# A Macaron block with routed experts on one core: shared expert moved into routing, expert rows scattered by token

## The chip, the cores and the metric

The kernel runs on one NeuronCore of one Trainium2 chip. The metric is the device time of one execution in microseconds (us). PE is TensorE, PEld its weight loads, DVE VectorE, ACT ScalarE, POOL GpSimd, SP the sync engine, which here only issues DMAs. An L with a number is a line of the kernel before.

## What is computed

4096 tokens (4 x 1024) of 256 float32 features pass a mixture-of-experts feed-forward, causal attention with 16 heads, and the same feed-forward again. The change touches the feed-forward alone:

```python
x = x + 0.5 * ffn(layernorm(x)); x = x + attention(layernorm(x)); x = x + 0.5 * ffn(layernorm(x))
# ffn(xf), T tokens, D = 256, 8 experts, TOP_K = 2, MOE_FF = 176, SHARED_FF = 352
scores = sigmoid(xf @ gate_w.T)
topk_w, topk_idx = top_k(scores, 2); topk_w = 2.5 * topk_w / topk_w.sum(-1)
shared_out = silu(xf @ shared_wg.T) * (xf @ shared_wu.T) @ shared_wd.T
h = silu(einsum('td,efd->etf', xf, exp_wg)) * einsum('td,efd->etf', xf, exp_wu)
all_out = einsum('etf,edf->etd', h, exp_wd)
routed_out = (topk_w[..., None] * all_out[topk_idx, arange(T)[:, None]]).sum(1)
return shared_out + routed_out
```

## The kernel before, in words

Tokens lie in 32 tiles of 128 partitions; X stays in SBUF through the whole kernel. Nearly float32 accuracy on TensorE comes from splitting each operand in a rounded high part (float32r, written by ACT) and the rest, the low part (DVE or POOL): every product is made in three passes, high x high, high x low, low x high (`split_passes`, L557). So each operand costs one pass of ACT and one of another engine.

A feed-forward (L92) has three stages with a barrier of all engines between them.

**Routing** (L120 to L550). Eight windows of four tiles: DVE normalises (L387), ACT stores the normalised rows to DRAM (L328), PE transposes them (L505), ACT and DVE split (L306, L392), PE makes the logits (L515, L522). Meanwhile ten weight units (two shared, eight experts) are loaded by SP through two raw buffers (L245, L249), rounded by ACT (L313, L322) and subtracted by POOL (L275, L283); all stay in SBUF. Then comes a chain on DVE, each link waiting for the one before (L417 to L477): the two best experts of each token, the counts (with two products, L540), and a slot for each token and choice in a list of 72 tiles of 128 rows sorted by expert. Eight rounds of one-hot matrices (DVE L485 and L489, ACT L353, POOL L293, PE L547) turn this into the token number of each slot.

**Expert stage** (L562). For each of the 72 tiles POOL gathers 128 rows of the normalised tokens by an indirect DMA (L604, four buffers, each waiting for the transposes of the tile four before), PE transposes (L701), six passes of 352 columns go up (L711), silu and product (L644, L672), two transposes of 88 columns (L720), six passes of 256 columns go down (L731), ACT copies (L623), and SP stores the tile at its slots (L613). The expert's weights are picked by a number loaded into a register.

**Shared stage** (L758). For each of the 32 token tiles: normalise and transpose again (L858, L938), twelve passes of 352 columns (L948), three transposes of h (L957), nine passes of 256 columns (L968). POOL gathers the two expert rows of each token from DRAM (L811, four tiles deep, waiting for the sum of the tile four before), DVE adds them with their weights (L879) and then the shared result (L886); the first feed-forward also takes the statistics for the next layer norm (L892), the second stores the result (SP, L821).

The order of the work on each engine is the order of the calls in its block; nothing is reordered.

Of the kernel before, what the change touches and what calls it, by code (L numbers as in the profile page):

```python
# [73 lines left out]
class Shapes:  # L74
    def __init__(self, x, w_up, w_down, gate):
# [9 lines left out]
        self.FH = self.FF // 2  # L85
# [3 lines left out]
        assert self.NS == 2 and self.NC == 2 and 2 * self.FH == self.FF and P // 2 < self.FH <= P and self.NT % 4 == 0 and self.NJ % 4 == 0  # L89


def feed_forward(nc, tag, S, X, ST, MV, ident, w_up, w_down, w_shared, gate, xn_dram, y_dram, out_dram):  # L92
# [4 lines left out]
    D, NT, NU, NS, FF, E, NJ, FH = S.D, S.NT, S.NU, S.NS, S.FF, S.E, S.NJ, S.FH  # L97
    NG = NT * TOP_K
    with ExitStack() as ctx:
# [3 lines left out]
        WUh = sb("WUh", [P, 2, NU * 2 * FF], F32R)  # L103
        WUl = sb("WUl", [P, 2, NU * 2 * FF], F32R)
        WDh = [sb(f"WDh{c}", [FH, E * D], F32R) for c in range(2)]
        WDl = [sb(f"WDl{c}", [FH, E * D], F32R) for c in range(2)]
        WSh = sb("WSh", [P, 3, D], F32R)
        WSl = sb("WSl", [P, 3, D], F32R)
        RSTD = sb("RSTD", [P, NT])
        W12 = sb("W12", [P, TOP_K, NT])  # L110
        slots_u = sb("slots_u", [P, TOP_K, NT], U32)
        tok_u = sb("tok_u", [P, NJ], U32)
        unit_i = sb("unit_i", [P, NJ], I32)
        X2 = X[:, :, :].rearrange("p t d -> p (t d)")
        MV2 = MV[:, :, :].rearrange("p t s -> p (t s)")
        NW = NT // 4
        assert NW <= NU <= NW + 2


        with ExitStack() as c1:  # L120
            sem = semaphores(nc, c1, f"{tag}1")

            def sb1(name, shape, dt=F32):
                return c1.enter_context(nc.sbuf_tensor(f"{tag}1_{name}", shape, dt))

            def ps1(name, shape):
                return c1.enter_context(nc.psum_tensor(f"{tag}1_{name}", shape, F32))

            XN = sb1("XN", [P, 2, 4, D])
            xh = sb1("xh", [P, 2, 2, 4 * P], F32R)  # L130
            xl = sb1("xl", [P, 2, 2, 4 * P], F32R)
            GW = sb1("GW", [P, 2, E])
            GWhl = sb1("GWhl", [P, 2, 2 * E], F32R)
            GWh0 = sb1("GWh0", [P, 2, 2 * E], F32R)
            LT = sb1("LT", [2 * E, 2, 4 * P])
            ADD = sb1("ADD", [2 * E, E])
            stage = sb1("stage", [P, 2, 4 * FF])
            stageD = sb1("stageD", [P, 2, 2, D])
            ps_x = [ps1(f"ps_x{i}", [P, 512]) for i in range(4)]
            ps_gate = ps1("ps_gate", [P, NT * E])  # L140
            ps_lt = [ps1(f"ps_lt{i}", [2 * E, 512]) for i in range(2)]
            ps_count = ps1("ps_count", [P, 2, E * NT])
            ps_tok = ps_x[0][:, 0:2 * NJ]
            SC = sb1("SC", [P, NT, E])
            SC2 = sb1("SC2", [P, NT, E])
            EQ = sb1("EQ", [P, NT, E])
            PR = sb1("PR", [P, NT, E])
            OH = sb1("OH", [P, TOP_K, NT, E])
            SEL = sb1("SEL", [P, E, NT], BF16)
            M12 = sb1("M12", [P, TOP_K, NT])  # L150
            PMAX = sb1("PMAX", [P, NT])
            DEN = sb1("DEN", [P, NT])
            prio_i = sb1("prio_i", [P, E], I32)
            prio = sb1("prio", [P, E])
            lower_t = sb1("lower_t", [P, P], BF16)
            ones_b = sb1("ones_b", [P, P], BF16)
            ones_f = sb1("ones_f", [P, E * NT])
            CUM = sb1("CUM", [P, E, NT])
            EXC = sb1("EXC", [P, E, NT])
            SLOT = sb1("SLOT", [P, E, NT])  # L160
            CNT = sb1("CNT", [P, E])
            CNTi = sb1("CNTi", [P, E], I32)
            NTI = sb1("NTI", [P, E])
            CT = sb1("CT", [P, E])
            BASE = sb1("BASE", [P, E])
            SL = sb1("SL", [P, TOP_K, NT])
            SLi = sb1("SLi", [P, TOP_K, NT], I32)
            Ri = sb1("Ri", [P, NG], I32)
            Ti = sb1("Ti", [P, NG], I32)
            RF = sb1("RF", [P, NG])  # L170
            TF = sb1("TF", [P, NG])
            row_i = sb1("row_i", [P, P], I32)
            row_f = sb1("row_f", [P, P])
            row_b = sb1("row_b", [P, P], BF16)
            par_i = sb1("par_i", [P, 1], I32)
            par_f = sb1("par_f", [P, 1])
            GE = sb1("GE", [P, NJ, E])
            UF = sb1("UF", [P, NJ])
            tile_of = sb1("tile_of", [P, NG])

            CH = NG // 8
            RSEL = sb1("RSEL", [P, 2, CH, P], BF16)
            EQT = sb1("EQT", [P, 2, CH, NJ], BF16)
            TSEL = sb1("TSEL", [P, 2, CH, 2, NJ], BF16)
            tokf = sb1("tokf", [P, 2 * NJ])

            raw_in = [sem("raw_in0"), sem("raw_in1")]
            gate_in = sem("gate_in")
            consts = sem("consts")
            chain = sem("chain")  # L190
            weights_hi = sem("weights_hi")
            split_w = sem("split_w")
            rstd_in = sem("rstd_in")
            rstd_out = sem("rstd_out")
            stats_done = sem("stats_done")
# [1665 lines left out]
```

## Time and profile before

| | us |
|---|---|
| median of 3 runs | 1437.1 (1436.49 to 1438.13) |
| the profiled execution | 1431.21 |
| its span, first to last instruction | 1429.5 |
| PE busy / DVE busy / ACT busy / POOL busy in it | 1219.7 / 1019.7 / 770.1 / 547.7 |
| mean granted clock of TensorE | 0.903 |

The profile comes from one execution. The granted clock is in parts of 2.4 GHz; 0.50 is 1.2 GHz. Busy time of POOL's indirect DMAs is the time in which it writes their descriptors, not that of the transfer. The span holds three parts that follow on each other: first feed-forward, attention, second feed-forward.

### The profile page before, as it was taken

The page shows a single profiled execution, that of the slowest core. Times are in us where ns is not written, and L with a number is a line of the kernel's source. Part 1 is how long each engine was busy: PE and PEld are TensorE (multiplying, and loading weights), DVE is VectorE, ACT ScalarE, POOL GpSimd, SP SyncE. Part 2 cuts the span into 40 slices and gives each one's busy share as a digit, 9 for nine tenths or more (in the row PEclk, how much of TensorE's full clock was granted, in tenths as well). Part 3 has the DMA queues.
Part 4 walks back from the last instruction along what each step waited for, and adds up shares of the span by engine and source line. Part 5 has one row for each costly group of instructions (what it writes and reads, how often), then busy time and mean ns, then how long its engine had stood idle before and what let it go on. Part 6 is the DMA issues. An engine that isn't in the chain of part 4 may idle for free. (4 is left out here: it accounts for less than half of the span.)

```text
span 1429.5 us, 42640 instructions
## 1 busy us (share of the span) xinstructions
PE 1219.7 (85%) x14356; PEld 938.2 (66%) x14357; DVE 1019.7 (71%) x2317; ACT 770.1 (54%) x1965; POOL 547.7 (38%) x745
## 2 busy tenths in 40 slices
PE   2817999899969849999998999997865299998998
PEld 1516999899958714555554555553743199998998
DVE  6594555479979688898886888981766845554887
ACT  2524556433336504887775777877544156564333
POOL 1555444245524401332332223222535554442554
PEclk9557999999979958999998999999975599998999
DMA  5602433322254492221221222101244034442333
GB/s 184 189 16 76 125 123 122 94 67 73 74 169 166 177 114 52 67 63 59 60 63 49 59 59 64 45 4 35 95 135 135 1 119 124 123 120 76 108 111 106
DMA packets 94745, 132.12 MB, mean 92 GB/s; under 512 B 15040, under 2 KB 79488, under 8 KB 94592
## 3 DMA queue, kind: packets, MB, share of 16 engines
q1 hardware_dynamic: 73088, 85.97, 21.0%
q0 software_dynamic: 13056, 35.67, 9.0%
q10 hardware_dynamic: 8448, 8.39, 1.7%
q8 instruction: 103, 1.69, 0.5%
q14 instruction: 50, 0.41, 0.1%
HBM read 81.35 MB, written 48.23 MB: 91 GB/s over the span
## 5 line engine op out<-in xcount | busy, mean ns | idle before, releaser
L1467 ACT ACTIVATE s_PR<-s_ps_b 128x512 f32<-128x512 f32 (+3 forms) x768 | 331.2, 496 | 144.8 <-PE s_ps_b L1583 139.9
L1489 DVE TENSOR_REDUCE s_MX<-s_ps_a 128x1 f32<-128x512 f32 (+3 forms) x608 | 358.3, 655 | 54.7 <-PE s_ps_a L1558 51.7
L1583 PE MATMUL s_ps_b<-s_QO,s_KO 99*32 99x512 bf16 (+3 forms) x3072 | 220.0, 329 | 9.2 <-issue 4.4
L1443 POOL TENSOR_SCALAR_AFFINE_SELECT s_PR<-s_PR 128x256 f32<-128x256 f32 x256 | 103.0, 405 | 311.6 <-ACT s_PR L1467 305.6
L1558 PE MATMUL s_ps_a<-s_KO,s_QO 96*32 96x512 bf16 (+3 forms) x3072 | 216.4, 339 | 2.7 <-issue 1.7
L604 POOL DMA_INDIRECT f_XG<-xn_scratch,f_tok_u x144 | 136.4, 947 | 165.5 <-PE f_ps_x L701 155.6
L811 POOL DMA_INDIRECT f_YG<-y_scratch,f_slots_u x128 | 121.0, 945 | 143.5 <-DVE X L886 87.9
L1600 PE MATMUL s_ps_o<-s_PR,s_VG 128*17 128x512 f32 (+3 forms) x1536 | 161.1, 488 | 1.0 <-POOL s_PR L1443 0.6
L1583 PEld LDWEIGHTS s_ps_b<-s_QO,s_KO 99*32 99x32 bf16 x3072 | 82.9, 96 | 91.0 <-ACT s_PR L1467 44.7
L657 DVE TENSOR_TENSOR f_xl<-f_ps_x,f_xh 128x256 fp32r<-128x256 f32 x144 | 61.1, 425 | 97.9 <-ACT f_xh L629 97.9
L1558 PEld LDWEIGHTS s_ps_a<-s_KO,s_QO 96*32 96x32 bf16 x3072 | 84.4, 99 | 69.6 <-DVE s_MX L1489 22.7
L844 ACT ACTIVATE f_SG<-f_ps_u 128x176 f32<-128x176 f32 x128 | 40.6, 317 | 142.3 <-PE f_ps_u L948 142.3
L1553 PE MATMUL s_ps_a<-s_neg,s_identb 128*32 128x128 bf16 (+2 forms) x1408 | 95.4, 253 | 25.1 <-DMA s_KO<-qk_scratch 22.1
L711 PE MATMUL f_ps_u<-f_WUh,f_xh 128*128 x288 | 106.4, 369 | 1.3 <-issue 1.0
L711 PE MATMUL f_ps_u<-f_WUl,f_xh 128*128 x288 | 94.1, 327 | 0.0
L711 PE MATMUL f_ps_u<-f_WUh,f_xl 128*128 x288 | 93.9, 326 | 0.0
L672 DVE TENSOR_TENSOR f_H<-f_SG,f_ps_u 128x176 f32<-128x176 f32 x144 | 48.7, 338 | 62.4 <-ACT f_SG L644 62.4
L948 PE MATMUL f_ps_u<-f_WUh,f_xh 128*128 128x352 f32 x256 | 91.2, 356 | 2.0 <-DVE f_xl L863 2.0
L731 PE MATMUL f_ps_y<-f_WDh,f_hh 88*128 x288 | 92.6, 321 | 0.1
L948 PE MATMUL f_ps_u<-f_WUh,f_xl 128*128 128x352 f32 x256 | 85.3, 333 | 0.0
L948 PE MATMUL f_ps_u<-f_WUl,f_xh 128*128 128x352 f32 x256 | 84.9, 332 | 0.0
L623 ACT ACTIVATE f_YS<-f_ps_y 128x256 f32<-128x256 f32 x144 | 55.3, 384 | 53.8 <-PE f_ps_y L731 53.8
(206 smaller groups left out, 3048.9 us busy)
## 6 DMA issues: line engine op xcount, KB each, us to landing
y_scratch<-f_YS SPq DMA_DIRECT2D x144, 128.0 KB, 1.7
qk_scratch<-p_QK SPq DMA_DIRECT2D x32, 384.0 KB, 2.6
s_QO<-qk_scratch SPq DMA_DIRECT2D x96, 128.0 KB, 2.8
s_KO<-qk_scratch SPq DMA_DIRECT2D x96, 128.0 KB, 2.8
xn_scratch<-f_XN ACTq DMA_DIRECT2D x16, 512.0 KB, 3.3
f_stage<-in_w_up SPq DMA_DIRECT2D x20, 352.0 KB
X<-in_x SPq DMA_DIRECT2D x4, 1024.0 KB, 9.4
x_scratch<-X SPq DMA_DIRECT2D x1, 4096.0 KB, 14.8
```

The source lines that it names most:

```text
L604: nc.gpsimd.indirect_dma_start(out=XG[:, j % 4, :], out_offset=None, in_=xn_dram[:, :], in_offset=bass.IndirectOffsetOnAxis(ap=tok_u[:, j: ...
L711: last = nc.tensor.matmul(ps_u[k % 2][:, 0:2 * FF], xs[a][:, k % 2, c * P:(c + 1) * P], W_up[b][:, c, ds(unit * (2 * FF), 2 * FF)], start= ...
L731: last = nc.tensor.matmul(ps_y[k % 2][:, 0:D], hs[a][:, k % 2, c * P:(c + 1) * P], W_down[b][c][:, ds((unit - NS) * D, D)], start=i == 0, ...
L811: nc.gpsimd.indirect_dma_start(out=YG[:, t % 4, c, :], out_offset=None, in_=y_dram[:, :], in_offset=bass.IndirectOffsetOnAxis(ap=slots_u[: ...
L948: last = nc.tensor.matmul(ps_u[s][:, 0:2 * FF], xs[a][:, k % 2, c * P:(c + 1) * P], W_up[b][:, c, s * 2 * FF:(s + 1) * 2 * FF], start=i == ...
L1443: nc.gpsimd.affine_select(out=tile, in_=tile, compare_op=ALU.is_ge, fill=0.0, base=0, pattern=[[0, 2], [1, P]], channel_multiplier=-1)\
L1467: nc.scalar.activation(PR[:, u // 2 % SLOTS, u % 2, 0:W - lo], ps_b[u % RING][:, lo:W], ACT.Exp, scale=SCALE).then_inc(exp_done, 1)
L1489: nc.vector.tensor_reduce(MX[:, h:h + heads, i, s], ps_a[slot][:, 0:heads * keys].rearrange("p (h n) -> p h n", h=heads), AX.X, ALU.max).t ...
L1553: nc.tensor.matmul(scores[strip, :, keys - P:keys], identb[:, strip], neg[:, 0:heads, :], start=True, stop=False, skip_group_check=True)
L1558: last = nc.tensor.matmul(ps_a[slot][strip, at:at + keys], QO[k][0:R, h, i * P + strip.start:i * P + strip.stop], KO[k][0:R, h, s * W:s * ...
L1583: last = nc.tensor.matmul(ps_b[u % RING][strip, lo:W], KO[k][0:RM, h, i * P + strip.start:i * P + strip.stop], QO[k][0:RM, h, hf * W + lo: ...
L1600: last = nc.tensor.matmul(ps_o[32 * h:32 * h + V1, lo:W], VG[k][:, i, h * V1:(h + 1) * V1], PR[:, (2 * n + h // 2) % SLOTS, h % 2, 0:W - l ...
```

## The change

**Expert tiles are scattered.** The token list now carries, for each slot, the token plus 4096 times the choice (a third column in the one-hot product marks used slots; unused ones get a spare row behind). POOL writes each finished expert tile by an indirect DMA to that row of a DRAM table. SP has nothing to do in the expert stage.

**The shared expert moves into the routing stage**, now `front_stage`. Its products are turned round: the weights are the stationary operand and 512 tokens move, so h comes out transposed and needs no transposes. The normalised x is transposed once, into the room where the expert weights will lie: window w occupies the place of expert w, whose weights are loaded through one raw buffer, and rounded and split, after window w is done. The gate work of all eight windows is ahead of or inside windows 0 and 1; the DVE chain lies in windows 2 and 3, the eight rounds of one-hot work in windows 4 to 7. ACT makes the ids of a round in nine operations; POOL makes none, but two of three low halves of h. SP stores the normalised rows.

**Five passes down.** h of an expert tile is cut 112 + 64 in place of 88 + 88. The low half of the 64 rows lies in partitions 64 to 127 under the high half, and the high weights stand twice, so one pass makes two products.

**The combine stage** has no products: SP loads windows of 512 tokens of both choices (RING = 4), DVE adds.

```diff
@@ expert stage, GpSimd
+            def scatter(j):
+                pool.wait_ge(y_copied, j + 1)
+                nc.gpsimd.indirect_dma_start(
+                    out=pairs_dram[:, :], out_offset=bass.IndirectOffsetOnAxis(ap=dst_u[:, j:j + 1], axis=0),
+                    in_=YS[:, j % 4, :], in_offset=None).then_inc(y_out[j % 4], 16)
+            for j in range(4):
+                gather(j)
+            for j in range(NJ + 3):
+                if j + 4 < NJ:
+                    gather(j + 4)
+                if j >= 3:
+                    scatter(j - 3)
             for k in range(4):
-                sp.wait_ge(y_out[k], 16 * (NJ // 4))
+                pool.wait_ge(y_out[k], 16 * (NJ // 4))
-            for j, k in steps(sp, NJ, 4):
-                sp.wait_ge(y_copied, j + 1)
-                sp.dma_start(y_dram[ds(j * P, P), :], YS[:, k, :]).then_inc(y_out[k], 16)
@@ expert stage, VectorE (h_low) and TensorE (down)
+                nc.vector.tensor_tensor(hl[:, k % 2, :], ps_h[k % 2][0:FA, 0:P],
+                                        hh[0:FA, k % 2, 0:P].bitcast(F32), ALU.subtract).then_inc(hl_done, 1)
+                nc.vector.tensor_tensor(hh[FB:2 * FB, k % 2, P:2 * P], ps_h[k % 2][0:FB, P:2 * P],
+                                        hh[0:FB, k % 2, P:2 * P].bitcast(F32), ALU.subtract).then_inc(hl_done, 1)
+                plan = ((hh[0:FA, b, 0:P], S.AH), (hh[0:FA, b, 0:P], S.AL), (hl[:, b, :], S.AH),
+                        (hh[:, b, P:2 * P], S.BH), (hh[0:FB, b, P:2 * P], S.BL))
@@ front stage
+    GATED = {-1: (0, 1), 0: (2, 3, 4), 1: (5, 6, 7)}
+    LAST_GATED = max(GATED)
+    COUNT_AT = LAST_GATED + 2
+    ROWS_AT = {4: (0, 1), 5: (2, 3), 6: (4, 5), 7: (6, 7)}
+    RING = 3
+            def up(w, m):
+                n = HC * w + m
+                at, used = CHUNKS[m]
+                for a in range(2):
+                    place = take("up" if a else "gate", n)
+                    for i, (c, x, b) in enumerate(split_passes(2)):
+                        last = nc.tensor.matmul(place[0:used, :], WU[b][:, c, a, at:at + used],
+                                                x_part(x, w)[:, c, :], start=i == 0, stop=i == 5)
+                    last.then_inc(up_done, 1)
@@ front stage, TensorE's order in window w
...
+                up(w, 0)
...
+                for n in ROWS_AT.get(w - 1, ())[1:2]:
+                    tokens(n)
+                if w == COUNT_AT:
+                    counts()
+                if w >= 1:
+                    for i in range(4):
+                        down(w - 1, i)
...
+                up(w, 1)
...
+                up(w, 2)
...
+                for n in ROWS_AT.get(w, ())[0:1]:
+                    tokens(n)
@@ front stage, SP: one raw buffer
+            def load_expert(e):
+                if e == 0:
+                    sp.wait_ge(shared_lo, 2 + HC)
+                else:
+                    sp.wait_ge(expert_lo, 3 * e)
@@ front stage, ScalarE
+            def token_ids(n):
+                act.wait_ge(onehot, n + 1)
+                if n >= 2:
+                    act.wait_ge(tok_done, n - 1)
+                nc.scalar.activation(TSEL[:, n % 2, :, 0, :], TSEL[:, n % 2, :, 2, :], ACT.Copy, scale=par_f[:, :])
+                for g in range(CH):
+                    last = nc.scalar.activation(TSEL[:, n % 2, g, 1, :], TSEL[:, n % 2, g, 2, :], ACT.Copy,
+                                                scale=float(n * CH + g))
+                last.then_inc(ids, 1)
@@ front stage, VectorE's order in window w
...
+                gated_h(w, 0)
...
+                if w >= 1:
+                    add_shared(w - 1)
+                if w == LAST_GATED + 1:
+                    choose(0)
+                if w == COUNT_AT:
+                    place()
+                for n in ROWS_AT.get(w, ())[0:1]:
+                    one_hot(n)
...
+                gated_h(w, 1)
...
+                if w == COUNT_AT:
+                    slots(0)
+                gated_h(w, 2)
...
+                h_low_2(w)
+                if w == LAST_GATED + 1:
+                    choose(1)
+                    weigh()
+                if w == COUNT_AT:
+                    slots(1)
+                    divide()
+                    units()
+                for n in ROWS_AT.get(w, ())[1:2]:
+                    one_hot(n)
@@ combine stage, SP and VectorE
+                    sp.dma_start(YG[:, w % RING, c, :, :],
+                                 pairs_dram[at:at + 4 * P, :].rearrange("(i p) d -> p i d", p=P)
+                                 ).then_inc(loaded[w % RING], 16)
+                nc.vector.scalar_tensor_tensor(X[:, t, :], YG[:, t // 4 % RING, c, t % 4, :], W12[:, c, t:t + 1], X[:, t, :],
+                                               ALU.mult, ALU.add).then_inc(x_done if c else mixed, 1)
```

## Rows read from the trace of the kernel before

**Rows 1.** Busy time by stretch: routing, expert, shared stage, second feed-forward.
```profile
core 0: us, PE busy (x) PEld busy (x) DVE busy (x) ACT busy (x) POOL busy (x), PEclk, DMA share, GB/s
18.70:117.07 98.37, 50.36 (x226) 33.47 (x226) 69.82 (x168) 38.93 (x83) 48.08 (x44) 0.61 0.33 98
117.07:281.20 164.13, 156.49 (x1152) 151.30 (x1152) 80.56 (x216) 93.73 (x289) 68.24 (x72) 0.97 0.38 116
281.20:404.82 123.62, 117.40 (x832) 115.38 (x832) 103.89 (x289) 43.12 (x128) 60.50 (x64) 0.97 0.24 68
1042.70:1429.50 386.80, 322.27 (x2210) 299.30 (x2210) 248.38 (x641) 175.92 (x500) 176.50 (x179) 0.87 0.35 107
```

**Rows 2.** Groups of lines, expert stage: busy, mean ns, idle before and its releasers.
```profile
L604 POOL DMA_INDIRECT f_XG<-xn_scratch,f_tok_u x68 | 64.3, 945 | 78.4 <-PE f_ps_x L701 78.1 <-issue 0.3
```

**Rows 3.** Timeline at the expert stage's start: start, us, engine, operation, idle before.
```profile
117.07 1.15 POOL L604 DMA_INDIRECT f_XG<-xn_scratch,f_tok_u  x1 [3.79 <-POOLq L64]
118.52 0.94 POOL L604 DMA_INDIRECT f_XG<-xn_scratch,f_tok_u  x1 [0.30 <-issue]
...
120.00 0.69 PE L701 MATMUL f_ps_x<-ident,f_XG 128*128 128x128 f32 x2 [5.46 <-DMA f_XG<-xn_scratch,f_tok_u]
...
126.86 0.94 POOL L604 DMA_INDIRECT f_XG<-xn_scratch,f_tok_u  x1 [0.81 <-PE f_ps_x L701]
```

**Rows 4.** Timeline: successive TensorE products with 512 and with 256 columns.
```profile
441.72 0.40 PE L1213 MATMUL p_ps_qk<-p_xh,p_Wh 128*128 128x512 f32 x1
...
441.95 0.40 PE L1213 MATMUL p_ps_qk<-p_xl,p_Wh 128*128 128x512 f32 x1
...
357.40 0.28 PE L968 MATMUL f_ps_y<-f_WSh,f_hl 128*128 128x256 f32 x1
...
357.51 0.28 PE L968 MATMUL f_ps_y<-f_WSh,f_hh 128*128 128x256 f32 x1
```

**Rows 5.** Groups of lines, first routing stage (0 to 117 us).
```profile
L275 POOL TENSOR_TENSOR f_WUl<-f_stage,f_WUh 128x704 fp32r<-128x704 f32 x10 | 17.0, 1697 | 33.6 <-ACT f_WDh L322 21.2 <-ACT f_WSh L322 12.4
...
L485 DVE TENSOR_TENSOR f_EQT<-f_row_f,f_TF 128x576 bf16<-128x576 f32 x8 | 12.7, 1582 | 0.0
...
L489 DVE TENSOR_TENSOR f_RSEL<-f_row_f,f_RF 128x1024 bf16<-128x1024 f32 x8 | 9.7, 1212 | 0.0
...
L353 ACT ACTIVATE f_TSEL<-f_EQT,f_par_f 128x576 bf16<-128x576 bf16 x8 | 6.2, 775 | 24.8 <-DVE f_EQT L485 24.8
L336 ACT ACTIVATE f_LT<-f_ps_lt 16x512 f32<-16x512 f32 x8 | 4.7, 586 | 9.9 <-PE f_ps_lt L515 9.9
```

**Rows 6.** Timeline of the first routing stage, rows picked over its second half.
```profile
67.81 0.39 SPq L245 DMA_DIRECT2D f_stage<-in_w_up  x1
...
71.66 0.79 ACT L313 ACTIVATE f_WUh<-f_stage 128x704 fp32r<-128x704 f32 x1 [1.48 <-DMA f_stageD<-in_w_down]
...
77.06 1.27 DVE L430 TENSOR_TENSOR f_SEL<-f_OH 128x256 bf16<-128x256 f32 x1
...
91.08 0.76 DVE L485 TENSOR_TENSOR f_EQT<-f_row_f,f_TF 128x576 bf16<-128x576 f32 x1
...
114.92 0.23 DVE L495 SCALAR_TENSOR_TENSOR f_tok_u<-f_tokf 128x72 uint32<-128x72 f32 x1
```

**Rows 7.** Groups of lines, first shared stage (281 to 405 us).
```profile
L879 DVE SCALAR_TENSOR_TENSOR X<-f_YG,f_W,X 128x256 f32 x48 | 22.9, 478 | 0.0
```

**Rows 8.** Timeline: VectorE's statistics back to back, and its first normalisations.
```profile
6.59 2.71 DVE L1808 BATCH_NORM_STATS2 ST<-X 128x6 f32<-128x256 f32 x8 [6.59 <-DMA X<-in_x]
...
23.93 1.71 DVE L387 TENSOR_SCALAR f_XN<-X,MV,f_RSTD 128x256 f32<-128x256 f32 x5
```

**Rows 9.** Busy time by stretch: cold expert start; output stage (two).
```profile
122.00:126.00 4.00, 3.72 (x16) 3.62 (x16) 1.19 (x3) 2.37 (x4) 2.78 (x3) 0.57 0.34 101
1028.00:1032.00 4.00, 3.39 (x26) 2.93 (x26) 3.45 (x11) 2.46 (x7) 0.00 (x0) 1.00 0.00 0
1000.00:1004.00 4.00, 3.47 (x18) 3.18 (x18) 0.51 (x2) 1.87 (x6) 2.26 (x1) 0.66 1.08 365
```

More of the change, by code:

```diff
@@ L84, in __init__ @@
         self.NJ = self.T * TOP_K // P + self.E
-        self.FH = self.FF // 2
+        self.FB = P // 2
+        self.FA = self.FF - self.FB
+        self.UH, self.UL = 0, 4 * self.FF
+        self.AH, self.AL, self.BH, self.BL = [8 * self.FF + n * self.D for n in range(4)]
+        self.BLOCK = 8 * self.FF + 4 * self.D
         self.HD = 16
@@ L101, in sb @@
             return ctx.enter_context(nc.sbuf_tensor(f"{tag}_{name}", shape, dt))
[L103 to L108, printed above, removed]
+        W = sb("W", [P, E, S.BLOCK], F32R)
         RSTD = sb("RSTD", [P, NT])
         W12 = sb("W12", [P, TOP_K, NT])
-        slots_u = sb("slots_u", [P, TOP_K, NT], U32)
+        dst_u = sb("dst_u", [P, NJ], U32)
@@ L437, in _, with place @@
                                                         ALU.mult, ALU.mult))
+            def place():
                 dve.wait_ge(pre_copied, 2)
@@ L541, in _ @@
                 nc.tensor.matmul(ps_count[:, 1, :], ones_b[:, :], sel, start=True, stop=True).then_inc(pre_done, 1)
-                for n in range(8):
-                    pe.wait_ge(rows, n + 1)
-                    pe.wait_ge(par_ids, n + 1)
-                    pe.wait_ge(tile_ids, n + 1)
-                    for g in range(CH):
-                        last = nc.tensor.matmul(ps_tok, RSEL[:, n % 2, g, :],
-                                                TSEL[:, n % 2, g, :, :].rearrange("p a j -> p (a j)"),
-                                                start=n == 0 and g == 0, stop=n == 7 and g == CH - 1)
-                    last.then_inc(tok_done, 1)
@@ L553, in feed_forward, with tokens @@
-        expert_stage(nc, tag, S, ident, WUh, WUl, WDh, WDl, tok_u, unit_i, xn_dram, y_dram)
-        shared_stage(nc, tag, S, X, ST, MV, RSTD, W12, slots_u, ident, WUh, WUl, WSh, WSl, y_dram, out_dram)
+            def tokens(n):
+                pe.wait_ge(rows, n + 1)
+                pe.wait_ge(ids, n + 1)
+                for g in range(CH):
+                    last = nc.tensor.matmul(ps_tok, RSEL[:, n % 2, g, :],
+                                            TSEL[:, n % 2, g, :, :].rearrange("p a j -> p (a j)"),
+                                            start=n == 0 and g == 0, stop=n == 7 and g == CH - 1)
+                last.then_inc(tok_done, 1)
@@ L557, in split_passes, with expert_stage @@
+            for i in range(4):
+                down(NW - 1, i)
+            tokens(7)
 def split_passes(n_chunks):
     return [(c, a, b) for c in range(n_chunks) for a, b in ((0, 0), (0, 1), (1, 0))]
-def expert_stage(nc, tag, S, ident, WUh, WUl, WDh, WDl, tok_u, unit_i, xn_dram, y_dram):
-    D, FF, NU, NS, NJ, FH = S.D, S.FF, S.NU, S.NS, S.NJ, S.FH
+def expert_stage(nc, tag, S, ident, W, tok_u, dst_u, unit_i, xn_dram, pairs_dram):
+    D, FF, E, NJ = S.D, S.FF, S.E, S.NJ
+    FA, FB = S.FA, S.FB
@@ L599, in _, with gather @@
         def _(pool):
-            for j in range(NJ):
+            def gather(j):
                 if j >= 4:
@@ L736, in _ @@
             U = 12
+            pe.wait_ge(cleared, 2)
             transpose_x(0, 0)
@@ L988, in attention @@
+                    nc.vector.bn_stats(ST[:, t, :], X[:, t, :])
+            for t in range(NT + 2):
+                if t < NT:
+                    add(t, 0)
+                if 1 <= t <= NT:
+                    add(t - 1, 1)
+                if t >= 2:
+                    statistics(t - 2)
 def attention(nc, S, X, ST, MV, ident, w_qkv, b_qk, b_v, w_out, b_out):
```

1069 lines of the change are left out of this document (536 added, 533 removed).

## The prediction

> **What bounds the kernel now.** I first cut the span at the stage borders [rows 1]. The first feed-forward takes 98.4 us for routing, 164.1 for the expert tiles and 123.6 for the shared expert with the combine: 386.1. The second takes 386.8. Attention between them isn't touched, so the question is what two times 386 becomes. TensorE is busy 156.5 of 164.1 us and 117.4 of 123.6 in the last two stages at a granted clock of 0.97: it bounds both. In routing it is busy 50 of 98 us, at 0.61; the end is set by VectorE's chain and eight rounds of one-hot work. Putting shared products there is sound in principle.
>
> Then I asked what POOL does in the expert stage. Its 68 gathers take 0.945 us each and it then waits, almost always for TensorE [rows 2]. Where it waits for nothing 0.30 us still goes by between two, so they start 0.94 + 0.30 = 1.25 us apart [rows 3]. So POOL uses 72 x 1.25 = 90 us of 164. That number decides the forecast.
>
> **Expert stage.** The change adds a scatter on POOL behind each gather and takes the plain store off SP's queue, which was idle otherwise. Now a tile costs TensorE 156.5 / 72 = 2.17 us [rows 1]. The fifth pass in place of a sixth saves one 256-column product, 0.115 us by the start-to-start distance [rows 4], so 2.06. POOL needs two indirect transfers a tile: 2 x 1.25 = 2.50. VectorE (80.6 us busy in the stage now, [rows 1]), whose subtraction is cut in two, and ScalarE (93.7) stay far below. POOL becomes the bound, and the saved pass (144 x 0.115 = 16.6 us over both halves, if TensorE were the bound) counts nothing. The stage: seven gathers go before the first scatter; the eighth waits for the fourth tile's transposes, 126.86 - 117.07 = 9.8 us [rows 3]. Then 144 - 7 = 137 transfers at 1.25 give 171.3. The last one's landing and the change of stage cost about 5 (TensorE had the first gather's rows 2.9 us after its start, and 1.9 lie between the last routing operation's end at 115.15 and the first gather [rows 3, 6]). Sum 186, against 164: **22 more**. No row shows a scatter's time on POOL. The nearest rows are the gathers: at least 0.945 without the gap, at most 1.15 + 0.30 = 1.45 (the first gather). I take 1.25, the row with the same number of rows and descriptors to write. The bounds are 22 us less a stage and 14 more.
>
> **Front stage, up to the first gather.** Start at 18.7. The x path for two windows and the shared weights come first: normalising begins at 23.9 [rows 8]; four rounds of transposes, copy and subtraction end near 31. ScalarE then rounds the shared weights (1408 columns and three of 256, about 2.6 us) and POOL subtracts (two of 704 columns at 1.70 [rows 5] and three of 256, some 5.7 as an estimate by columns), both after the loads. First shared product at 37: 18.3 us.
>
> TensorE's work. A window of 512 tokens has 36 products of 512 columns at 0.234 and 36 of 256 at 0.115 [rows 4]: 12.56 us, eight times 100.5. Gate work of the other six windows: 8 transposes (0.11 each, an estimate from the 256-column product), 4 products of 512 and 4 tiny ones, 2.3 each, 13.8. Token products 64 x 0.10 = 6.4, counts 0.3. Sum 121; 4.9 of it lies behind the last up product, so 116. A cold clock at the start: 2.
>
> Stalls, by walking the orders of the queues (ring of three PSUM buffers, a 512-column pass on ScalarE 0.59 [rows 5], 0.7 on VectorE as an estimate from 0.478 for 256 columns [rows 7]). Windows 0 and 1: logits wait for transposes, copy and subtraction of their window, 5.5 us. Window 3: the counts wait for SEL, which sits in VectorE's chain behind the low half of h: 3.8. Into window 4: the chain from SEL's end at 78.3 to the first one-hot operation at 91.1 took 12.7 us in one piece [rows 6]; it is now cut in three, but its last 4.2 us stand ahead of the next gated product, and two down products wait for the shared add behind that: 5.3. Windows 5 to 7: after the last up product come gate 0.7, rounding 0.6, low half 0.7, one-hot 0.8, then nine ScalarE operations for the ids (0.775 for 576 columns [rows 5] and eight of 0.2), 5.7 us in all, while TensorE has only 2.8 us of other work: 2.9 each, 8.6. Stalls together 23, so the last up product ends at 37 + 116 + 2 + 23 = 178.
>
> The tail. Expert weights pass through a single raw buffer, so the eighth is loaded only when the seventh is split. From the last up product: ids 6.6 (late by 0.9), expert 6's down part on ScalarE 1.1 and on POOL 0.8, load 3.9 (67.81 to 71.66, [rows 6]), rounding 0.8, then POOL 1.7 + 1.5, and 1.9 to the first gather: 18. The token ids are ready earlier, so this is exposed. **Front 177** (18.3 + 116 + 2 + 23 + 18), to 196.
>
> What hides: the shared add, the normalised rows' store now on SP, expert splits on POOL (about 5.7 of 15 us a window). If that cover goes they cost directly. The first one-hot operation, with POOL idle, took 0.76 us [rows 6], while the mean of all eight, most of them beside POOL's work, is 1.58 [rows 5]; POOL now works in every window. The Trainium skill (SBUF — State Buffer, the reading of its port diagram) says a GpSimd operation and a VectorE operation with two SBUF inputs lock each other out for the whole instruction; by that rule normalising, low halves and the chain would wait up to 1.7 us each time, some 10 us a front on top of the sum. The trace's mean agrees in kind.
>
> **Combine stage.** No TensorE. Per tile two multiply-adds (0.478 long [rows 7], start to start about 0.08 less, as eight statistics took 2.71 [rows 8]): 0.40, and 0.34 for statistics. 64 x 0.40 + 32 x 0.34 = 36.5, with 5 for the first loads and 1.5 at the end 43. The second half has no statistics but stores 4.2 MB beside 8.4 MB of loads: 12.6 MB at 365 GB/s [rows 9] 34.5, plus 5 and 2.5: 42. It was 123.6 with the shared work: this is where the gain is.
>
> **Sum.** First half 177 + 186 + 43 = 406, against 386.1: 20 more. Second 177 + 186 + 42 = 405, against 386.8: 18 more. The profiled execution took 1431.2 (span 1429.5); plus 39 gives 1470. The median of the runs is 5.9 higher, 1437.1, so I forecast **1476**.
>
> **Rivals.**
> A. The front flows. If the orders leave TensorE never waiting, 23 us fall away in each: 1476 - 46 = 1430. For it: TensorE has 14 to 20 us of work a window, and the other engines less. Against: the ids' chain is longer than its cover by two operations. Chance 0.13, split between same and faster.
> B. Faster: POOL's 0.30 us gap overlaps once each transfer has its own semaphore wait, so a pair costs 1.89, below TensorE's 2.06. The stage would be 72 x 2.06 = 148, plus 9 to start and 5 to end, 162: 24 less each, 1428. It decides below 2.06 a pair; the total turns faster below about 2.25. Against: the second gather waited for nothing and still kept the gap [rows 3]. Chance 0.08; with A as well 1382, 0.02.
> C. The front is worse by the port: 10 to 20 us each, 1496 to 1516. Chance 0.10.
> D. TensorE's clock falls in the expert stage, since it idles 0.44 us in each 2.50. Around the cold start it was granted 0.57 [rows 9]. At 1.2 GHz a tile would be up to 4.1 us, the stage 306, the total up to 1716. Against: the output stage ran at 2.4 GHz (1.00) with TensorE busy 3.39 of 4 us [rows 9]; 82% is close to that. The Trainium skill (TensorE: Matmul & The Clock Gate, Part 1) says the array is throttled by default and activity releases it; by that rule such a tile loop, fully busy once slow, would be released again, and the time would lie between. Chance 0.05.
> E. The forecast, 0.62, alone 1445 to 1510.
>
> About 0.2%, 3 us, is what a measurement of this kernel tells from no change. Faster: half of A, B, both: 0.15. Same 0.05. Slower 0.80. The range 1430 to 1520 takes in the scatter's upper bound (2 x 14) and C, and ends at A; D and B lie outside.
>
> **What to look for.** POOL's idle time in the expert stage gone, with transfers 1.25 apart and TensorE waiting for gathers, confirms the main step; a TensorE that still waits for nothing refutes it. First gather near 196 and combine near 43 confirm the rest. A scatter under 1.0 us start to start, or a first gather before 175, makes the forecast wrong.

## The result and the profile after

The changed kernel took 1586.4 us (median of four runs, 1582.5 to 1590.0) against 1437.6 beside it: a ratio of 1.1035, with a 95% interval of 1.1008 to 1.1062. It is slower, as forecast, but by 149 us where 39 were expected, and 66 above the upper end of the range. Its profiled execution took 1586.4, its span is 1584.5, which is 155 above the span before.

The stages again by stretch, in the columns of [rows 1]: front, expert tiles, combine, and the whole second feed-forward.

```profile
core 0: us, PE busy (x) PEld busy (x) DVE busy (x) ACT busy (x) POOL busy (x), PEclk, DMA share, GB/s
18.80:208.27 189.47, 150.58 (x802) 121.16 (x802) 103.26 (x220) 78.97 (x189) 54.52 (x53) 0.92 0.17 51
208.27:445.85 237.58, 198.32 (x1080) 162.38 (x1080) 91.27 (x289) 92.78 (x288) 140.91 (x144) 0.89 0.25 80
445.85:487.75 41.90, 0.00 (x0) 0.00 (x0) 35.85 (x96) 0.00 (x0) 0.00 (x0) 0.50 0.62 200
1117.40:1584.50 467.10, 351.77 (x1882) 286.62 (x1882) 220.44 (x572) 172.52 (x477) 195.34 (x196) 0.84 0.28 89
```

Forecast were 177, 186, 43 and 405. So the front missed by 12.5, the combine by 1, and the expert stage by 51.6. The second half, 467.1 against 405, missed by as much (62). The rest adds up: 63 + 62 over, less 8.2 by which attention was shorter (629.7 against 637.9, not looked into), is 117, and 1586.4 - 1470 = 116.

Was POOL the bound of the expert stage? The groups of lines on the page, both halves:

```profile
L867 POOL DMA_INDIRECT f_pairs<-f_YS,f_dst_u x144 | 142.1, 987 | 138.1 <-ACT f_YS L887 108.0
...
L860 POOL DMA_INDIRECT f_XG<-xn_scratch,f_tok_u x144 | 139.7, 970 | 49.3 <-issue 39.0
...
L921 DVE TENSOR_TENSOR f_xl<-f_ps_x,f_xh 128x256 fp32r<-128x256 f32 x144 | 61.1, 424 | 119.3 <-ACT f_xh L893 93.4
```

The prices are near what I took (0.97 and 0.99 us, against 0.945 in [rows 2]), and "issue" is the 0.30 us gap of [rows 3], now paid wherever POOL has nothing to wait for. But POOL idled 108 us ahead of scatters, waiting for ScalarE's copy of a finished tile. The timeline of POOL, stage one:

```profile
248.97 0.99 POOL L867 DMA_INDIRECT f_pairs<-f_YS,f_dst_u  x1 [0.30 <-issue]
250.27 0.97 POOL L860 DMA_INDIRECT f_XG<-xn_scratch,f_tok_u  x1 [0.30 <-issue]
251.54 0.99 POOL L867 DMA_INDIRECT f_pairs<-f_YS,f_dst_u  x1 [0.30 <-issue]
252.83 0.97 POOL L860 DMA_INDIRECT f_XG<-xn_scratch,f_tok_u  x1 [0.31 <-issue]
256.11 0.99 POOL L867 DMA_INDIRECT f_pairs<-f_YS,f_dst_u  x1 [2.31 <-ACT f_YS L887]
```

A pair starts 2.57 us after the pair before (248.97, 251.54), then one comes 4.57 later. In the middle of the stage the mean is 3.31 us. Why does ScalarE come late? The same 6 us on TensorE and ScalarE, from the timeline of all engines:

```profile
250.11 0.38 ACT L887 ACTIVATE f_YS<-f_ps_y 128x256 f32<-128x256 f32 x1 [0.45 <-PE f_ps_y L1001]
...
250.96 0.32 PE L979 MATMUL f_ps_u<-f_W,f_xl 128*128 x1
...
252.08 0.38 ACT L893 ACTIVATE f_xh<-f_ps_x 128x256 fp32r<-128x256 f32 x1 [1.59 <-remote]
...
253.97 0.32 PE L979 MATMUL f_ps_u<-f_W,f_xl 128*128 x1
254.97 0.32 ACT L908 ACTIVATE f_SG<-f_ps_u 128x176 f32<-128x176 f32 x1 [2.51 <-PE f_ps_u L979]
255.19 0.38 ACT L899 ACTIVATE f_hh<-f_ps_h 112x256 fp32r<-112x256 f32 x1
...
255.72 0.32 PE L987 MATMUL f_ps_h<-ident,f_H 128*112 128x128 f32 x1 [1.43 <-DVE f_H L940]
```

ScalarE's silu at 254.97 needs the up product that ended at 250.96 + 0.32 = 251.28, and ScalarE itself was free from 252.46. It stood 2.5 us before work that, by the records of TensorE, was there. Counting every ScalarE operation of the stage that starts over 0.4 us after both its product's recorded end and its own predecessor gives 49 such **late starts**, 61 us together, the longest 4.0. The kernel before has none. On VectorE, which waits for ScalarE, and on TensorE, which waits for VectorE, there are none. (Apart from 7.0 us of POOL's idle time no other engine waits here for a fresh signal of TensorE.)

Is the signal late, or ScalarE? The trace also records when a semaphore is raised. Usually that is 0.01 us behind the end of the last product of a group. But the groups that end at 251.28, 251.50, 252.28, 252.65 and 254.29 (two of up products, and one each of transposes of h, down products and transposes of x) raise their four semaphores at 254.95, 254.99, 255.06, 255.10 and 255.18: five in 0.23 us. The starts of one group's six up products alone spread over 0.88 us, so the work was done before; its signals were held and came in a burst, and ScalarE starts 0.02 us behind the first. This had no place in my forecast.

### The profile page after: what moved, and what is told of

The parts are those of the page before. It is cut to its first block and busy times, and to the rows that moved or that the text cites. A ratio compares the mean times of both kernels' runs of the same rounds, so it can differ in the third digit from the quotient of the medians.

```text
span 1584.5 us, 38969 instructions
## 1 busy us (share of the span) xinstructions
PE 1271.9 (80%) x13700; PEld 906.2 (57%) x13701; DVE 966.6 (61%) x2179; ACT 762.9 (48%) x1919; POOL 585.2 (37%) x779
## 5 line engine op out<-in xcount | busy, mean ns | idle before, releaser
L867 POOL DMA_INDIRECT f_pairs<-f_YS,f_dst_u x144 | 142.1, 987 | 138.1 <-ACT f_YS L887 108.0
L1001 PE MATMUL f_ps_y<-f_W,f_hh 112*128 (+1 forms) x576 | 163.3, 353 | 19.1 <-DVE f_hh L928 17.8
L979 PE MATMUL f_ps_u<-f_W,f_xh 128*128 x576 | 166.5, 374 | 5.8 <-issue 4.7
L860 POOL DMA_INDIRECT f_XG<-xn_scratch,f_tok_u x144 | 139.7, 970 | 49.3 <-issue 39.0
L728 PE MATMUL f_ps_u<-f_W,f_WUh 128*128 128x512 f32 (+1 forms) x384 | 135.0, 419 | 1.6 <-DVE f_H L505 1.3
L1001 PEld LDWEIGHTS f_ps_y<-f_W,f_hh 112*128 112x128 f32 (+1 forms) x576 | 107.1, 206 | 50.9 <-issue 32.9
L344 POOL TENSOR_TENSOR f_hl<-f_H,f_hh 128x512 fp32r<-128x512 f32 x32 | 42.7, 1333 | 196.4 <-ACT f_hh L386 196.4
L908 ACT ACTIVATE f_SG<-f_ps_u 128x176 f32<-128x176 f32 x144 | 46.1, 320 | 142.1 <-PE f_ps_u L979 107.4
L979 PEld LDWEIGHTS f_ps_u<-f_W,f_xh 128*128 128x128 f32 x576 | 105.5, 211 | 13.9 <-issue 13.2
L979 PE MATMUL f_ps_u<-f_W,f_xl 128*128 x288 | 99.9, 347 | 0.0
```

The source lines that it names most:

```text
L728: last = nc.tensor.matmul(place[0:used, :], WU[b][:, c, a, at:at + used], x_part(x, w)[:, c, :], start=i == 0, stop=i == 5)
L860: nc.gpsimd.indirect_dma_start(out=XG[:, j % 4, :], out_offset=None, in_=xn_dram[:, :], in_offset=bass.IndirectOffsetOnAxis(ap=tok_u[:, j: ...
L867: nc.gpsimd.indirect_dma_start(out=pairs_dram[:, :], out_offset=bass.IndirectOffsetOnAxis(ap=dst_u[:, j:j + 1], axis=0), in_=YS[:, j % 4, ...
L979: last = nc.tensor.matmul(ps_u[k % 2][:, 0:2 * FF], xs[a][:, k % 2, c * P:(c + 1) * P], W_at[:, ds(unit * S.BLOCK + (S.UL if b else S.UH) ...
L1001: last = nc.tensor.matmul(ps_y[b][:, 0:D], h, W_at[0:h.shape[0], ds(unit * S.BLOCK + at, D)], start=i == 0, stop=i == len(plan) - 1)
```

## The experiments

Theories at the start: N, the narrow products (the fifth down pass reads 64 rows, the second transpose of h writes 64) slow TensorE and make its signals late; Q, the scatter stands in POOL's in-order queue ahead of the next gathers; C, the clock. "Stage" is the first expert stage, from its first gather to the first load of the combine; 72 tiles. "Us a tile" is the mean distance of TensorE's up products of tiles 20 to 50. Late starts are counted in the first stage. Each of e1 to e10 and of g1 to g3 is a single execution; e11 has four and f1 to f4 two each, and those of one kernel lie within 11 us.

**Four side by side: wider products, and no scatter.** e1 zeroes 64 rows of weights and reads them:

```
-  (hh[:, b, P:2 * P], S.BH), (hh[0:FB, b, P:2 * P], S.BL))
+  (hh[:, b, P:2 * P], S.BH), (hh[:, b, P:2 * P], S.BL))
+  nc.vector.memset(W[FB:2 * FB, :, S.BL:S.BL + D].bitcast(F32), 0.0)
```

> The fifth down pass reads all 128 rows instead of 64; the other 64 rows of its weights are zeros. The result is the same and the pass still streams 256 columns. Theory N (narrow products): in the expert stage of the changed kernel the 64-row pass starts 0.21 us behind its predecessor and the next product 0.31 behind it, where other 256-column passes start 0.115 apart, and ScalarE often starts 1 to 4 us after the recorded end of the product it waits for, which it never does in the kernel before. If the 64-row pass causes both, the expert stage falls from 237.6 to POOL's bound of about 186 us (72 x 2.57) and the total from 1586 to about 1485. If the 64-column transpose causes the late starts, only 0 to 20 us a stage go: 1550 to 1586. Rival Q (POOL's order): the scatter blocks the gathers behind it in POOL's queue; this edit then changes nothing, 1580 to 1590.

e2 widens H by 64 zero columns and transposes them with the others:

```
-  nc.tensor.transpose(ps_h[k % 2][0:FB, P:2 * P], H[:, k % 2, FA:FF], ident[:, :])
+  nc.tensor.transpose(ps_h[k % 2][:, P:2 * P], H[:, k % 2, FA:FA + P], ident[:, :])
```

> The second transpose of h takes 128 columns of h instead of 64 (64 of them zeros); the 64-row pass stays. Theory N with the 64-row pass as its cause: no change, 1580 to 1590. N with the 64-column transpose as the cause: toward 1485. Rival Q (POOL's order): no change.

e3 is both:

> Both edits together: no product of the expert stage uses fewer than 65 rows or columns. Theory N whichever of the two it is: expert stage about 186 us by POOL's 2.57 us a tile, POOL waits for ScalarE hardly at all, no late starts on ScalarE, total near 1485. Rival Q: unchanged, 1580 to 1590. Rival C (TensorE's clock, 0.89 granted in the stage): unchanged or slightly better, over 1560.

e4 takes the scatter away:

```
-  scatter(j - 3)                                  # POOL
+  sp.wait_ge(y_copied, j + 1)                     # SP
+  sp.dma_start(pairs_dram[ds(j * P, P), :], YS[:, k, :]).then_inc(y_out[k], 16)
```

> The scatter is left out: SyncE stores each tile by slot, so POOL only gathers, and the combine reads rows in the wrong places. The narrow products stay. Theory N: TensorE and the late signals bound the stage; it stays well above 200 us (about 210 to 237), total 1530 to 1586. Rival Q: with no scatter in POOL's queue the stage falls to TensorE's 2.33 us a tile, 165 to 175 us, total 1450 to 1470.

Measured: 1501.2, 1497.9, 1501.9 and 1469.4 us; stages of 194.2, 194.8, 194.0 and 178.6; no late start in any. The stage of e3, and its POOL:

```profile
210.10:404.10 194.00, 163.60 (x1080) 145.80 (x1080) 92.60 (x291) 93.25 (x288) 140.99 (x144) 0.97 0.31 98
```

```profile
249.38 0.97 POOL L861 DMA_INDIRECT f_XG<-xn_scratch,f_tok_u  x1 [0.30 <-issue]
250.66 0.99 POOL L868 DMA_INDIRECT f_pairs<-f_YS,f_dst_u  x1 [0.30 <-issue]
251.95 0.97 POOL L861 DMA_INDIRECT f_XG<-xn_scratch,f_tok_u  x1 [0.30 <-issue]
253.23 0.99 POOL L868 DMA_INDIRECT f_pairs<-f_YS,f_dst_u  x1 [0.30 <-issue]
```

This is the stage that I forecast, at 2.57 us a tile where I had 2.50: POOL never waits. It looked as if any one of the edits cured the late signals, which no single cause explains.

**Controls.** The changed kernel as it is, and with the zeros written but not read:

> The changed kernel, unaltered, beside the others. Rows widened, columns widened, both widened and the scatter left out each took the stage from 237.6 to 194, 195, 194 and 179 us, which no single cause among the three explains. Theory P (a pair of conditions: 64-row pass and 64-column transpose and the scatter must all be there): this run repeats 1583 to 1590, stage near 238. Rival L (the late signals of TensorE belong to one build or chip and not to the products' shape): about 1500 here, stage near 195, without late starts of ScalarE.

> The zeros are written into the unused rows as in the kernel with the full-row pass, but the fifth pass still reads 64 rows, so all products of the changed kernel are as they were. Theory P: the stage stays near 238 us and the total near 1586. Rival L' (something incidental, that any small edit moves): about 195 us and 1500.

1593.8 and 1582.9, stages 239.3 and 238.8, 43 and 45 late starts. That spoke for P and was misleading, as the repetition below shows.

**What the narrow pass costs by itself.** The kernel before with its last down pass over 64 of 88 rows:

```
-  hs[a][:, k % 2, c * P:(c + 1) * P], W_down[b][c][:, ds((unit - NS) * D, D)]
+  hs[a][0:n, k % 2, c * P:(c + 1) * P], W_down[b][c][0:n, ds((unit - NS) * D, D)]   # n = 64 if i == 5 else FH
```

> The kernel before, with the last of its six down passes of a tile over 64 of 88 rows (24 rows of the low part are left out of the result). Nothing else is narrow, POOL only gathers. If a 64-row pass between full ones costs TensorE 0.3 us (0.1 ahead, 0.2 behind), a tile goes from 2.17 to about 2.45 us and the total from 1432 to 1432 + 144 x 0.29 = 1474, with less arithmetic than before. If the gap beside it is TensorE waiting for other engines in the changed kernel only, 1430 to 1437.

1480.9 against 1432.0: 49 slower with less arithmetic. TensorE's timeline of one tile:

```profile
200.64 0.28 PE L732 MATMUL f_ps_y<-f_WDh,f_hh 88*128 x1
200.75 0.28 PE L732 MATMUL f_ps_y<-f_WDl,f_hh 88*128 x1
200.96 0.38 PE L732 MATMUL f_ps_y<-f_WDh,f_hl 64*128 x1
201.27 0.44 PE L701 MATMUL f_ps_x<-ident,f_XG 128*128 128x128 f32 x2
```

The 88-row passes start 0.11 apart, the 64-row one 0.21 behind its predecessor, and what follows it 0.31 behind. A tile takes 2.45 us against 2.16 before. That is 144 x 0.29 = 42 of the 49; late starts: none. The Trainium skill (TensorEngine Tiling (Array Packing), Key Properties) says that a change of tiling mode drains TensorE, and its table of configurations has 64 rows as a mode of their own; these rows agree. A product with 64 columns shows no such cost: in e4 the next product starts 0.03 us behind the 64-column transpose (302.50, 302.53), in e6, the next experiment, 0.02 behind the 128-column one (302.03, 302.05).

**All wide, no scatter.** Both widened, with the plain store:

> Full rows, full columns, and the plain store in place of the scatter (the combine then reads rows in the wrong places). No narrow product, no scatter: TensorE is the bound at five passes. If the mode change is what the 64-row pass costs, a tile falls from 2.33 us (plain store with narrow products, stage 178.6) to 2.06: stage 157 to 160, total 1469 - 2 x 20 = 1429. If the 64-row pass costs nothing by itself: 1469.

1452.5, stage 167.2:

```profile
211.90:379.10 167.20, 157.48 (x1080) 145.17 (x1080) 92.65 (x290) 93.05 (x288) 68.33 (x72) 0.97 0.37 114
```

Against e4 (178.6) that is 11.4 us a stage for the two widened shapes, but 2.25 us a tile and not the 2.06 of my sum. e4 runs at 2.34, so in this kernel the narrow shapes cost 0.09 us a tile and not the 0.29 of e5. The kernel before has six passes and runs at 2.16. So with POOL out of the way the fifth pass still gives nothing back: TensorE's first up product starts 0.35 us behind the transposes (300.50, 300.85), where it was 0.14 (201.29, 201.43 before). What exactly it waits for there I did not separate.

**Does it take the scatter? Does the place of the narrow pass matter?** e9 puts a second gather into an unused buffer where the scatter stood:

```
-  out=pairs_dram[:, :], out_offset=...dst_u[:, j:j + 1], in_=YS[:, j % 4, :]
+  out=XD[:, j % 4, :], in_=xn_dram[:, :], in_offset=...tok_u[:, j:j + 1]
```

> The narrow products stay, SyncE stores by slot, and POOL issues a second gather of the same rows into an unused buffer at the place, and behind the wait, where the scatter stood (the combine reads rows in the wrong places). POOL's load and order are those of the changed kernel, but nothing is scattered. If the late signals of TensorE come from both narrow shapes together with a TensorE that is paced by POOL: late starts of ScalarE again, 3.3 us a tile, stage near 238, total near 1590. If the scatter itself is needed (its reads of the tile buffer or its writes): no late starts, 2.57 a tile by POOL, stage near 194, total near 1500.

e10 puts the 64-row pass first of the five:

> The changed kernel with the 64-row pass first of the five, right behind the 64-column transpose, so that the two narrow products are neighbours. If only their presence in a tile counts: 3.3 us a tile and 1580 to 1595. If it counts that TensorE changes shape twice a tile with full products between: with one narrow stretch a tile the late starts go, 2.57 a tile, near 1500.

1605.7 and 1600.0, stages of 245.7 and 245.2, with 44 and 40 late starts. Nothing needs to be scattered, and the order of the passes is not it.

**Two raw buffers in the front, with full columns.**

```
-  sp.wait_ge(expert_lo, 3 * e); sp.dma_start(RAW[...]).then_inc(expert_in, 16)
+  if e >= 2: sp.wait_ge(expert_lo, 3 * e - 3)
+  sp.dma_start(RAWE[:, e % 2, ...]).then_inc(expert_in[e % 2], 16)
```

> Full columns in the transpose, and two raw buffers for the expert weights in the front instead of one. The tail from the last shared up product to the first gather was 16.9 us (191.4 to 208.3), the last 9 of them loading and splitting expert 7 behind expert 6. With the load done early it should be 4 us shorter in each half: 1498 - 8 = 1490. If POOL and ScalarE are the bound there in any case, 1 us or nothing: 1496 to 1498. In neither case does it reach the kernel before.

From the last up product to the first gather went 191.8 to 204.9, 13.1 us, against 191.5 to 208.5, 17.0, with one buffer (f3 below): 3.9 less, as expected. But the total was 1588.0 (ratio 1.1036, 1.1003 to 1.1068), with 42 late starts, although e2, with the same full columns, had had none. Theory P had to be tested again.

**The same four again, side by side.**

> The first four experiments ran side by side and gave stages of 194, 195, 194 and 179 us; later the changed kernel gave 239 and full columns with two raw buffers 243, in other comparisons. So the late signals may hang on something outside the kernel. Here the changed kernel and the three widened ones run side by side. Theory P (products' shapes): this one 1583 to 1595 with late starts, the three others near 1500. Rival X (something outside the kernel that was different in the first comparison): all four near 1590, or all four near 1500.

> Full rows in the fifth pass, again. Theory P: near 1500 as at first, no late starts. Rival X: as the changed kernel beside it, whatever that is. If the 64-row pass alone makes late starts: 1500 here and in the one with both wide, 1590 in the other two.

> Full columns in the second transpose, again. Theory P: near 1500. Rival X: as the changed kernel beside it. If the 64-row pass alone makes late starts: near 1590.

> Full rows and full columns, again. Theory P, or the 64-row pass alone: near 1500, 2.57 us a tile by POOL. Rival X: as the changed kernel beside it. 1590 here beside 1590 for the others would clear the shapes of the late signals altogether, and leave TensorE paced by POOL's two transfers.

1597.7, 1592.7, 1599.3 and 1590.1, ratios 1.105 to 1.111 with intervals that overlap; 40, 45, 40 and 47 late starts. The stage of the one with both wide:

```profile
207.80:446.80 239.00, 184.99 (x1080) 165.74 (x1080) 91.79 (x291) 91.80 (x288) 141.32 (x144) 0.86 0.25 80
```

```profile
L868 POOL DMA_INDIRECT f_pairs<-f_YS,f_dst_u x72 | 71.3, 990 | 67.5 <-ACT f_YS L888 52.8 <-issue 14.7
```

It is the kernel of e3 to the letter, 45 us longer in this stage. **The shapes are cleared of the late signals**; theory P falls. What was different for e1 to e3 lies outside the kernels.

**Is it TensorE's waiting, or POOL's second transfer?** g1 keeps one transfer and slows VectorE by 1152 columns a tile; g2 cuts the second transfer to 16 rows; g3 gives POOL slack:

```
g1 +  nc.vector.memset(IDLE[:, :], 0.0)                      # once a tile
g2 -  out=XD[:, j % 4, :], in_offset=...tok_u[:, j:j + 1]
g2 +  out=XD[0:16, j % 4, :], in_offset=...tok_u[0:16, j:j + 1]
g3 -  gather(j + 4); scatter(j - 3)                         # rings of 4
g3 +  gather(j + 6); scatter(j - 5)                         # rings of 6
```

> All products wide, POOL only gathers, SyncE stores by slot (the combine reads rows in the wrong places), and VectorE writes 1152 columns of an unused buffer once a tile, about 1.1 us, so that VectorE and not POOL sets the tile. TensorE then waits 0.3 to 0.5 us in each tile, as it does behind two transfers. If TensorE's waiting alone makes its signals late: late starts of ScalarE, well over 3 us a tile, total over 1560. If it takes two POOL transfers a tile: none, about 2.5 to 2.7 us a tile, total 1480 to 1510.

> All products wide, SyncE stores by slot (the combine reads rows in the wrong places), and POOL's second transfer of a tile is a gather of 16 rows in place of 128. If POOL's time for a transfer goes by its rows, a pair takes about 0.97 + 0.30 + 0.3 to 0.5 + 0.30, under TensorE's 2.25: stage near 167, no late starts, total 1450 to 1460. If most of it is the same for any number of rows, 2.3 to 2.57 a pair. Late starts here, with TensorE not paced by POOL, would lay them to the second transfer itself; total 1560 or more.

> All products wide, the scatter as in the changed kernel, but six row buffers and six result buffers instead of four, gathers six tiles ahead and the scatter two tiles later in POOL's queue. It computes the reference. If POOL's own idle (108 us before scatters) is lost because its queue stands still while TensorE's signals are late, half of it comes back: about 2.85 us a tile, total 1530 (or 1500 where there are no late signals). If the late signals cost TensorE's chain the time whatever POOL does, 3.2 to 3.3 a tile and about 1590.

The three stages, one fence for each kernel:

```profile
211.90:393.30 181.40, 165.23 (x1080) 145.96 (x1080) 146.70 (x363) 92.89 (x288) 68.18 (x72) 0.97 0.36 105
```

```profile
211.60:448.40 236.80, 185.51 (x1080) 165.68 (x1080) 90.67 (x290) 90.40 (x288) 130.34 (x144) 0.87 0.29 85
```

```profile
212.00:437.50 225.50, 172.30 (x1080) 152.92 (x1080) 90.52 (x291) 88.77 (x288) 140.77 (x144) 0.93 0.27 84
```

g1: 1480.4, no late start at 2.36 us a tile. VectorE set that pace, though less slowly than meant (2.5 to 2.7), and TensorE waited for it: waiting alone isn't the cause at this pace. Nor is a slow tile as such: e5 ran at 2.45 without late starts. One transfer a tile at 2.57 or more was not tried. g2: 1588.2, 52 late starts, 3.23 a tile. The 16-row gather is enough. Its price on POOL, and its waits:

```profile
L872 POOL DMA_INDIRECT f_XD<-xn_scratch,f_tok_u x72 | 61.3, 851 | 76.1 <-ACT f_YS L901 61.7 <-issue 14.4
```

16 rows cost 0.85 us, 128 rows 0.96: a transfer's price on POOL hardly goes by its rows. g3: 1566.4, 3.00 a tile, and POOL's wait for the copy falls from 52.8 us to 8.3:

```profile
L868 POOL DMA_INDIRECT f_pairs<-f_YS,f_dst_u x72 | 71.1, 987 | 26.9 <-issue 18.3 <-ACT f_YS L888 8.3 <-DMA f_pairs<-f_YS,f_dst_u 0.3
```

Yet the stage shortens only from 239.0 to 225.5, not to 205. POOL's in-order queue (rival Q) passes on 13.5 of the 45 us. The rest I put to TensorE's own chain, whose buffers are two deep and which stops while ScalarE waits; no run shows that by itself. No version here beats the kernel before (1432 to 1440).

**Counted over all of them:** with one indirect transfer of POOL a tile (the kernel before, e4, e5, e6, g1) there were no late starts. Of the fifteen results with two, counting repetitions, twelve had 40 to 62 of them in the first stage, and e1 to e3 none. g1 to g3 ran on the same chip as e1 to e4, so the chip alone does not explain those three.

One thing does set them apart in the record. TensorE raises 288 signals in a stage. For e1, e2 and e3 the trace holds 287 of them, for e4, which ran beside them, 288. In the first stages of the twelve with late starts it holds 217 to 258, and records of ScalarE's and VectorE's signals are missing as well. Missing records alone do not make late starts: e6 has 220 and g1 270, and neither has one. But the same file, as e3 and as f4, is fast with 287 records and slow with 245.

## Why the prediction was wrong, point by point

**What bounds, and the direction: right.** The sum's expert term said that POOL's two transfers replace TensorE as the bound. e3 shows it alone: 194.0 us with POOL never waiting, against 186. The step's 2.50 a pair was 2.57 (0.97 + 0.99 + 2 x 0.30); over 68 pairs that is 5 of the 8 us. The total of e1 to e3, 1498 to 1502, lies within my range.

**The step that failed** is "the stage: 137 transfers at 1.25 give 171.3", which takes POOL to run without a wait because nothing it waits for is near its limit. In the changed kernel it waited 108 us over both halves ahead of scatters. In place of 2.50 us a tile the runs showed 3.2 to 3.3 (3.0 with rings of six). Late signals of TensorE are what ScalarE, and through it POOL, waits for. Shown is where they appear (in twelve of fifteen results with two indirect transfers a tile, even when the second has 16 rows, no matter the shapes and their order), and where not (one transfer). Not shown is the mechanism, nor why e1 to e3 were free of them. I can't price that in advance from the trace of before: nothing in it shows such a signal.

**Whether the recording takes part** stays open. The Trainium skill (NOTIFIC — the notification-queue block, Interfaces) says that back pressure from the block that writes trace records can stall an engine when an internal FIFO fills; no run here shows that block. What the runs show is the count above: of the results with two transfers a tile, the three without late starts have whole records, and the twelve with them do not. The record has a span and a granted clock for every execution that was timed, so none is known to have run without the profiler; how long the changed kernel takes then, and whether that is nearer to e3's 1502 us than to 1586, no run says.

**The saved pass: counted at nothing, rightly, but for one reason too few.** POOL hides it. Beyond that the 64-row shape costs 0.1 ahead and 0.2 behind in e5, more than the 0.115 it saves. With one transfer the five passes of e4 take 2.34 us a tile, and 2.25 with full shapes in e6, against 2.16 for six before. Rival B (a pair at 1.89, then 2.06 a tile) would have ended at 2.34 and not at 1428 in all. B itself is refuted by the 0.30 us, which stays between all transfers.

**Front, 189.5 against 177.** The first shared product started at 39.0 (37); the last up product ended at 191.4 (178); the tail was 16.9 (18). So 2 of the 12.5 us are at the start and 11.4 in the middle. The stalls up to the last up product sum to 18.9, less than my 23: SEL 4.7 (3.8), down behind the shared add 3.1 (5.3), ids 1.7, 1.9 and 1.9 (2.9 each). The term that I mis-sized is the clock: 2 us, once, at the start. TensorE ran slowly six times. Granted clock in two of these stretches and in one between:

```profile
60.70:64.00 3.30, 3.30 (x9) 2.61 (x10) 0.11 (x1) 0.29 (x1) 0.00 (x0) 0.56 0.67 231
133.00:136.00 3.00, 3.00 (x11) 2.38 (x11) 2.63 (x3) 0.92 (x2) 1.46 (x1) 0.62 0.00 0
50.00:54.00 4.00, 4.00 (x26) 2.97 (x26) 1.10 (x2) 1.82 (x4) 1.27 (x2) 1.00 0.52 155
```

Nine products in 3.3 us against 26 in 4, at a granted 0.56 and 0.62 (mostly the lower of the two levels). The whole stretches at the lower level are 60.2 to 63.6, 104.6 to 111.4, 128.5 to 135.3, 162.6 to 166.0 and 179.7 to 183.1, each behind a wait of TensorE (0.7, 4.7, 3.1, 1.9 and 1.9 us); waits of 1.1, 0.7 and 1.7 us at 67.8, 83.5 and 143.0 had none behind them. In them 512-column products start 0.43 apart in place of 0.234, and 256-column ones 0.21 in place of 0.115. Added up, that is 1.9 us at the start (by the same distances; the trace has no clock before 43.1) and 1.4, 2.4, 2.9, 1.6 and 1.5 later: 11.7, where I had 2. So a wait could be paid twice here, once as idle time and once in the clock behind it.

**Combine, 41.9 and 37.8 against 43 and 42: right** by its steps, the second within 4: its 12.6 MB moved at 333 GB/s over the whole 37.8 us, so 3.3 of the 7.5 us that I added at its ends were left.

**The rivals.** A: no, the stalls came. C (10 to 20 us a front, by the port): the size was that (12.5 us), the reason mostly not: the clock took 9.7 more than I gave it. The locking is there: the one-hot of 1024 columns took 2.32 us beside a POOL subtraction and 1.21 alone,

```profile
186.66 1.47 POOL L344 TENSOR_TENSOR f_hl<-f_H,f_hh 128x512 fp32r<-128x512 f32 x1 [5.82 <-ACT f_hh L386]
186.90 2.32 DVE L610 TENSOR_TENSOR f_RSEL<-f_row_f,f_RF 128x1024 bf16<-128x1024 f32 x1
...
194.61 1.21 DVE L610 TENSOR_TENSOR f_RSEL<-f_row_f,f_RF 128x1024 bf16<-128x1024 f32 x1
```

1.11 more, where POOL's operation overlapped it by 186.66 + 1.47 - 186.90 = 1.23; the rule of the Trainium skill (SBUF — State Buffer) that I weighed fits this row. How much of the front it cost no run separates. D (the clock falls in the expert stage, up to 1716): the granted clock was 0.89, but e3, where POOL is the bound and TensorE is idle 30.4 of 194.0 us, 0.42 a tile, kept 0.97. It fell with the late signals (0.86 in f4, 0.93 in g3), so I read it as following them and not as the cause. The forecast was given 0.62 and D 0.05: the measured time lies where only D reached, for another reason. The chances by outcome did not follow from those of the rivals either: half of A, B and both give 0.165 for faster and not 0.15, half of A 0.065 for the same, and the rest 0.77 for slower and not 0.80. And POOL's subtraction of the shared weights comes to 5.3 us by its own terms and not to 5.7. Neither changes the forecast.

## What to carry to other kernels

Moving a transfer onto the engine that already issues the gathers makes that engine the bound at the sum of its fixed costs, and rows saved in it give next to nothing; price it per transfer. Packing a pass into 64 rows to save another can cost more than it saves, so look at the start-to-start distance on both sides of the first product with an odd shape. Price a wait of TensorE together with the slow stretch that can follow it. And repeat a "cure" beside the uncured kernel before believing it: three edits that each seemed to win some 85 us won at most 7.6 when run beside it, where the two executions of the uncured kernel are 10.2 apart.

## What was not expected of the hardware

- ScalarE starts up to 4.6 us (g2; 4.0 in the changed kernel) after the recorded end of the product it waits for, 40 to 62 times in 72 tiles, in twelve of fifteen results with two indirect transfers a tile; the mean tile goes from 2.57 to 3.2 or 3.3 us. Up to five signals come in one burst of 0.23 us.
- A 64-row product among full ones: 0.21 us ahead and 0.31 behind against 0.11 to 0.12 (e5); the kernel before loses 49 us by leaving rows out.
- An indirect transfer of 16 rows holds POOL for 0.85 us, one of 128 for 0.96, with 0.30 between any two that wait for nothing.
- Five stretches at the lower clock in one front stage, 23.9 us in all and each behind a wait of 0.7 to 4.7 us, cost 9.8 us.
